# The first six slots by halves of time, the feed-forward statistics moved among the slots, and the first head prepared during the output projection

## The reference

```python
x = LN(x + hyena(x))          # LN, W_in (1536 x 512), 3-tap filter, three kinds x0 x1 v,
                              # v*x1, long convolution over T, * x0, W_out
x = LN(x + heads(ctx, x))     # 32 heads of 8 rows: products k_i*v_j of ctx, long convolution
                              # over L = 512, contracted with x
x = LN(x + ffn(x))            # bitlinear(512->2048), gelu, bitlinear(2048->512)
# bitlinear: rms = rsqrt(max(mean(w*w), eps)); w_quant = clip(round(w*rms), -1, 1) / rms
#            x_quant = clip(round(x*127/max|x|)) ...
```

## Time and profile before

| quantity | value |
|---|---|
| three timed runs | 1128.77, 1130.29, 1130.85 us |
| profiled execution, its own time | 1128.79 us |
| its span | 1127.0 us |
| mean granted TensorE clock | 0.977 |
| TensorE (matmul), VectorE, ScalarE, GpSimd busy | 93%, 72%, 52%, 52% of the span |

### The profile page before, as it was taken

The page is one execution under the profiler, slowest core; times in us unless marked ns, Lnnn a source line. Parts: engine busy times, 40 slices in busy tenths (PEclk is TensorE's granted clock), DMA queues, the critical chain, the costliest instruction groups (busy, mean ns, idle before and its releaser), DMA issues.

```text
span 1127.0 us, 16879 instructions
## 1 busy us (share of the span) xinstructions
PE 1052.1 (93%) x5316; PEld 643.6 (57%) x5316; DVE 816.0 (72%) x1531; ACT 589.4 (52%) x710; POOL 586.0 (52%) x1136
## 2 busy tenths in 40 slices
PE   1799899999999987969999999999999999999985
PEld 1455455544545533556676767676766666666652
DVE  6978786696565546857777878787878787777762
ACT  2355444203444463825565656565656565666654
POOL 2301310131000003559878787878787878788770
PEclk9899899999999998989999999999999999999997
DMA  8233445455244584332121222212131313131101
GB/s 236 93 89 113 146 140 172 147 177 177 92 133 150 150 328 147 122 112 58 57 84 58 74 67 65 74 57 83 50 89 47 93 47 93 47 90 50 47 10 29
DMA packets 95215, 115.23 MB, mean 102 GB/s; under 512 B 19584, under 2 KB 52352, under 8 KB 93632
## 3 DMA queue, kind: packets, MB, share of 16 engines
q1 hardware_dynamic: 95168, 114.63, 33.5%
HBM read 80.90 MB, written 33.70 MB: 102 GB/s over the span
## 4 chain that ended last, share of the span: by engine, by line
PE 53%; POOL 2%; ACT 1%; DVE 1%; issue 0%; POOLq 0%; DVEq 0%
PE conv_bank L1255 26%; PE hq_bank L1289 10%; PE ff_bank L1317 5%; PE back_bank L1317 5%; PE ctx_bank L1230 1%; PE ff_bank L1282 1%; PE hq_bank L1282 1%; PE back_bank L1240 1%; PE back_bank L1269 1%; PE ctx_bank L1300 1%; POOL up L1626 0%; POOL dn L1627 0%; POOL up L1629 0%; ACT o L1415 0%; POOL att L1639 0%
## 5 line engine op out<-in xcount | busy, mean ns | idle before, releaser
L752 DVE SCALAR_TENSOR_TENSOR conv_all<-u,taps,conv_all 128x1024 f32<-128x1024 f32 x96 | 126.4, 1317 | 97.9 <-ACT conv_all L624 96.1
L1255 PE MATMUL conv_bank<-block_diag 128*128 128x288 f32 x640 | 175.6, 415 | 8.8 <-PEq L265 6.0
L1255 PE MATMUL conv_bank<-kv,block_diag 128*128 128x288 f32 x640 | 171.7, 408 | 0.0
L938 POOL TENSOR_SCALAR r_rstd<-r_meanvar 128x1 f32<-128x1 f32 x32 | 13.0, 407 | 258.3 <-DVE r_meanvar L776 258.3
L616 ACT ACTIVATE u<-slot_bank,bias,unscale 128x1024 f32<-128x1024 f32 x48 | 57.9, 1207 | 164.9 <-PE slot_bank L466 161.3
L1255 PEld LDWEIGHTS conv_bank<-block_diag 128*128 128x128 f32 x640 | 120.1, 194 | 40.6 <-issue 6.6
L1626 POOL TENSOR_TENSOR up<-z_up 128x384 f32<-128x384 f32 x128 | 127.7, 998 | 27.9 <-DVE z_dn L1502 27.0
L1255 PEld LDWEIGHTS conv_bank<-kv,block_diag 128*128 128x128 f32 x640 | 117.8, 190 | 30.9 <-DVE z_dn L1502 0.5
L1490 DVE TENSOR_TENSOR z_up<-conv_bank,qx 128x512 f32<-128x512 f32 x128 | 87.7, 685 | 55.6 <-PE conv_bank L1255 43.3
L1557 DVE TENSOR_REDUCE g_max<-g 128x1 f32<-128x512 f32 x128 | 87.3, 683 | 54.8 <-ACT g L1430 54.8
L1289 PE MATMUL hq_bank<-x_lo,hq_t 128*128 128x512 f16 x512 | 124.6, 388 | 1.6 <-ACT hq_t L1397 1.6
(11 more groups left out here) (175 smaller groups left out, 1880.5 us busy)
## 6 DMA issues: line engine op xcount, KB each, us to landing
...
res<-in_x SPq DMA_DIRECT2D x32, 256.0 KB, 2.9
x_scratch<-res SPq DMA_DIRECT2D x32, 256.0 KB, 2.0
block_diag<-in_ctx SPq DMA_DIRECT2D x32, 256.0 KB, 3.4
block_diag<-ssm_scratch SPq DMA_DIRECT2D x32, 256.0 KB, 3.1
x_tok<-x_scratch SPq DMA_DIRECT2D x32, 256.0 KB, 3.7
```

Source lines behind the costliest of these rows:

```text
L752: ins = nc.vector.scalar_tensor_tensor(out=acc, in0=u[:, t0 + tap:t0 + tap + T // 2, :].rearrange("p t b -> p (t b)"), scalar=w["taps"][:, ...
L1255: last = nc.tensor.matmul(view(conv_bank[tb % 2][:, hh, :], 0, (ROW64, T // 2), (1, PAIRS)), toep[:, head.buf, (tb - sb_) * P:(tb - sb_ + ...
```

## The change

**Start.** Quad 0 is loaded first, then W_in's first group, gamma and beta, quad 1, and the small vectors, which now come as rows of 12 partitions in three DMAs and are transposed by TensorE (`turn_columns`, `copy_columns`). x of the first half is normalized by ScalarE (`norm_first`, 16 activations), with the shift made by GpSimd. The first six slots are ordered X1, V, X0 for the first eight time steps, then X1, V, X0 for the last eight; slots 0 and 3 take their columns quad by quad. Slots 0 to 2 write three separate `u` tiles, and ScalarE copies two columns of time from these for slots 4 and 5. `turn_quad(2)` and `turn_quad(3)` follow slots 1 and 2, W_in group 1 slot 4, and W_out slot 5.

**Feed-forward weights.** All eight parts are loaded and squared during the slots of the second half, in two buffers, and loaded a second time for rounding. The totals and the root are made at slots 18 to 21. Rounding is one activation on ScalarE (a multiplication and a large constant added) and one clip on VectorE; TensorE transposes the low 16 bits of the float32 in place, and the copy subtracts the offset. Transposition runs at t = 1 to 8 instead of 7 to 14.

**Output projection.** `load_res` is issued three steps ahead instead of two. ctx, Toeplitz rows and x1 of heads 0 and 1 are loaded ahead of step 0.

**First head.** ctx is transposed after t = 11, its products are made after t = 12, and the first two blocks of its convolution run at the end of `hyena_block`. `turn_x1(0)` is the first work of TensorE in `heads_block`.

The diff, cut to its core. Tables and the order of the slots:

```diff
-    def slot_of(s):
-
+    def slot_of(hf, s):
+
+        if hf == 0 and s < 2 * len(KIND_AT):
+            return 0, s % 3, s // 3
         return *PAIRS_OF_SLOTS[s // 2], s % 2
...
+        u_first = [u[:, :, :], v_ct[:, 6:T, :], view(x_quad[:, :, :, :], 0, (P, T // 2 + TAPS - 1), (1, P))]
...
-        TOTAL_AT = {3: 0, 5: 1}
-        RMS_AT = {4: 0, 6: 1}
-        ROUND_AT = {5 + i: i for i in range(2 * PARTS)}
-        PART_AT = {7 + i: i for i in range(2 * PARTS)}
-        TURN_AT = {3: 1, 10: 2, 14: 3}
-        SUM_AT = {0: 1, 5: 2, 10: 3}
...
-        SCALE_AT = {2: 1, 7: 2, 12: 3}
-        WOUT_AT = 2
+        SQUARE_AT = {1: 0, 3: 1, 5: 2, 8: 3, 10: 4, 12: 5, 15: 6, 17: 7}
+        TOTAL_AT, SUM_MATRIX_AT, MEAN_AT, INVERSE_AT = 18, 19, 20, 21
+        ROUND_AT = {21: 0, 23: 1}
+        CLIP_AT = {i - 1: i for i in range(2, 2 * PARTS)}
+        PART_AT = {1 + i: i for i in range(2 * PARTS)}
+        CTX_AT, PAIRS_AT = 11, 12
+        TURN_AT = {4: 1, 10: 2, 14: 3}
+        SUM_AT = {5: 2, 10: 3}
...
+        SCALE_AT = {3: 1, 7: 2, 12: 3}
+        WOUT_AT = 5
```

SyncE, the set-up and the second half:

```diff
+                load_quad(0)
                 load_w_in(0)
                 for src, tile in ((dram["ln_beta"], beta_bc), (dram["ln_gamma"], gamma_bc)):
                     sp.dma_start(tile, bass.AP(src.tensor, 0, [[0, P], [1, D]])).then_inc(gb_loaded, 16)
-                load_quad(0)
+                load_quad(1)
+                sp.dma_start(cols_raw[:, 0:P], dram["b_in"].rearrange("(n p) -> n p", p=P)).then_inc(cols_loaded, 16)
...
+                load_quad(2)
+                load_quad(3)
...
+                def load_stat(i):
 
                     if i < 2:
                         sp.wait_ge(x_turned, DC * (HALF * NQ - 1 + i))
+                    else:
+                        sp.wait_ge(squared, i - 1)
+                    sp.dma_start(part_target(i, part_raw[i % 2]), part_source(i)).then_inc(stat_loaded[i % 2], 16)
...
+                        load_stat(0)
+                        load_stat(1)
+                        regroup(hf, 0)
+                        load_stat(2)
+                        load_stat(3)
+                        load_stat(4)
+                        bring_back(hf, 0)
+                        load_stat(5)
+                        regroup(hf, 1)
+                        load_stat(6)
+                        load_stat(7)
+                        bring_back(hf, 1)
+                        regroup(hf, 2)
                         load_part(0)
                         load_part(1)
...
+                        bring_back(hf, 2)
+                        regroup(hf, 3)
+                        load_part(2)
+                        load_part(3)
+                        bring_back(hf, 3)
+                        for i in range(4, 2 * PARTS - 1):
                             load_part(i)
+
+
+                        sp.wait_ge(ch_full, 4 * HALF * DC)
...
+                            sp.dma_start(early["ctx_tok"][:, h, :], dram["ctx"][:, heads, :]).then_inc(early["ctx_loaded"][h], 16)
+                            sp.dma_start(early["toep"][:, h, :], toeplitz(dram, h)).then_inc(early["toep_loaded"][h], 16)
+                            sp.dma_start(early["x1_tok"][:, h, :], dram["x1_scratch"][:, heads, :]).then_inc(early["x1_loaded"][h], 16)
...
-                        if R + 2 < HALF * T:
-                            load_res(R + 2)
+                        if R + 3 < HALF * T:
+                            load_res(R + 3)
```

TensorE:

```diff
                 pe.wait_ge(ident_made, 2)
+                turn_quad(0)
+                turn_columns()
                 turn_w_in(0)
-                turn_quad(0)
+                slot(0, 0, (0,))
                 turn_quad(1)
                 for hf in range(HALF):
                     for s in range(NSLOT):
-                        slot(hf, s)
+                        slot(hf, s, (0, 1) if hf + s > 0 else (1,))
                         if hf == 0:
-                            if s == 0:
-                                turn_quad(2)
-                                turn_quad(3)
+                            if s in (1, 2):
+                                turn_quad(s + 1)
...
                     for j in range(DC):
-                        pe.wait_ge(*turn_read(KINDS + DC * NQ + j - 4))
+                        if j == 0:
+                            pe.wait_ge(w_lo_done, 2 * KINDS)
+                            pe.wait_ge(x_lo_done, DC * NQ)
...
+                def convolve_first(tb):
+
+                    if tb == 0:
+                        pe.wait_ge(early["toep_loaded"][0], 16)
+                        pe.wait_ge(early["kv_done"], 1)
+                        pe.wait_ge(part_done, 2 * 2 * PARTS)
+                    for sb_ in range(tb + 1):
+                        for hh in range(2):
+                            last = first_conv(nc, early, turn_bank[2 * tb + hh][:, :, :].rearrange("p a b -> p (a b)"), tb, sb_, hh)
+                    last.then_inc(early["conv_full"], 1)
...
+                for tb in range(2):
+                    convolve_first(tb)
```

ScalarE:

```diff
-                    if pr == 0 and n >= 2:
+                    u_here = u_first[kind] if n < 3 else u
+                    if n == 3 or n >= 6 and pr == 0:
                         act.wait_ge(conv_done, n)
+                    elif 4 <= n < 6:
+
+                        act.wait_ge(conv_done, n)
+                        act.wait_ge(u_done, kind + 1)
+                        nc.scalar.copy(u[:, T // 2:T // 2 + TAPS - 1, :], u_first[kind][:, T // 2:T // 2 + TAPS - 1, :])
...
+                def norm_first(Q):
+                    act.wait_ge(x_shifted, Q + 1)
+                    for t in range(QUAD):
+                        x = quad_buf(Q)[:, t, :]
+                        last = nc.scalar.activation(x, x, ACT.Identity, scale=rstd[:, Q, t:t + 1], bias=shift[:, Q, t:t + 1])
+                    last.then_inc(x_normed_first, 1)
...
+                    nc.scalar.activation(part_raw[i], part_raw[i], ACT.Copy, scale=rms[:, m:m + 1], bias=LOW_HALF).then_inc(rounded, 1)
...
+                norm_first(0)
+                split_hi(0)
                 scale_w_in(0)
                 copy_w_in(0)
-                split_hi(0)
+                norm_first(1)
                 split_hi(1)
+                norm_first(2)
```

VectorE:

```diff
+                def clip_part(i):
+
+                    dve.wait_ge(rounded, i + 1)
+                    nc.vector.tensor_scalar(part_raw[i], part_raw[i], LOW_HALF - 1.0, LOW_HALF + 1.0, ALU.max, ALU.min).then_inc(clipped, 1)
...
+                norm_quad_stats(0)
                 sum_beta(0)
-                norm_quad_stats(0)
+                norm_quad_stats(1)
                 measure_w_in(0)
-                norm_quad(0)
-                norm_quad_stats(1)
+                copy_columns()
+                split_lo(0)
                 split_w_lo(0)
-                split_lo(0)
-                norm_quad(1)
+                nc.vector.memset(u_first[2][:, 0:TAPS - 1, :], 0.0).then_inc(u_zeroed, 1)
+                make_biases(0)
                 norm_quad_stats(2)
                 split_lo(1)
                 norm_quad_stats(3)
-                norm_quad(2)
-                norm_quad(3)
+                sum_beta(1)
```

SyncE and TensorE in `heads_block`:

```diff
                 for i in range(4):
                     sp.wait_ge(early["res_stored"][i], 16 * (HALF * T // 4))
-                load_x1(Head(0))
-                load_x1(Head(1))
...
                     h1, h2 = n.back(1), n.back(2)
+                    if n.c == 0:
+                        turn_x1(n)
                     if n.exists():
                         convolve(n, 0, [0])
```

362 lines of the change are left out of this document (200 added, 162 removed).

## The result

The changed kernel took 1111.59, 1113.58, 1114.43 and 1115.59 us, median 1114.0, against 1130.6 for four runs of the kernel before: a ratio of 0.9858 with a 95% interval of 0.9844 to 0.9872, 16 us less. (Behind a ratio, square brackets hold its 95% interval.) The forecast was 1101, the range 1092 to 1112. The profiled execution took 1111.59 us, its span is 1109.6 us, its mean clock 0.984; it is 17.2 us shorter than the profiled execution before, where the forecast had 28.1. Measured again in a later comparison (e14) it took 1108.29 to 1116.76 in six runs, median 1112.23, ratio 0.9839 [0.9815, 0.9863].

What follows compares the result with a forecast made beforehand. TensorE was taken as the bound, busy 1052.1 of 1127.0 us, leaving its idle and lower-clock time to win. Terms 5.2 + 0 + 14.3 + 2.4 + 6.2 = 28.1 off 1128.8 gave 1100.7, said as 1101; range 1092 to 1112.

Steps and rivals of the forecast that it cites:

- Start, 5.2: Before slot 8: x loaded first and norms off VectorE let slot 8 start at 88.0 against 93.25, 5.2 us gained.
- Queued behind these waits are only later slots: After the start's waits: nothing but later slots is delayed, and V's regrouping has time, so the 5.2 us stays.
- slots of the second half, 0: Second half's slots: squares, rounding and clips moved there fit into idle engine time; cost 0, bounds 0 to 4 us.
- With a square 4.5, so nothing shows: Second half's slots: ScalarE's share with a square is 4.5 us, under TensorE's 5.2 per slot, so no cost.
- rival D: SP's in-order queue: load_stat waits for a square, regroupings start late and TensorE waits for v; 1136 us, chance 0.04.
- Output projection, 14.3: Second half's output projection: 64 out-products without the wait for the weights' total take 64.2 us; gain 14.3.
- Products out of the tail, 2.4: End of the output projection: the first head's products (0.4 and 2.28 us) leave the tail; gain 2.4.
- Three tiles of slack: Residual loads in the output projection: tiles 0 to 2 are there ahead, which spoke against rival C's loss of 8 us.
- rival C: Output projection still waits for data, parts and head loads queued ahead of residuals; loses 8 us, 1109, chance 0.09.
- First head, 6.2: After the change of block: with x1 there, VectorE's first multiplication comes after 1.9 us, not 8.1; gain 6.2, bounds 3 to 6.5.
- B: Start gives nothing or costs a little: half clock after gaps, VectorE-to-ScalarE turns in slots 3 to 5; 1108 us, chance 0.13.
- E: First head is held by another load or engine, and its 6.2 us is lost; 1107 us, chance 0.06.

Runs made afterwards that it cites:

- e1: The changed kernel with every tile of the first block at its address in the kernel before, no instruction different: 1108.66 us, ratio 0.9813.
- e2: The kernel before with its first-block tiles at the changed kernel's addresses, no instruction different: 1134.33 us, ratio 1.0028.
- e15: The changed kernel with SyncE's order at a step turned round, store_res(R) ahead of load_res(R + 3): 1107.51 us, ratio 0.98.
- e16: The changed kernel with old addresses, squares of parts 0 and 2 later, three TensorE pauses filled with transposes, and stores ahead of residual loads: 1102.19 us, ratio 0.9746.
- e17: The changed kernel with old addresses, squares of parts 0 and 2 later and three pauses filled, residual loads still ahead of stores: 1106.2 us, ratio 0.9782.
- e11: The changed kernel at the old addresses, plus 20 unread identity transposes on TensorE behind the first head's early blocks: 1105.07 us, ratio 0.9802.

## Why the prediction was wrong

The sign was right, and so were the places and the sizes of the two large terms; the sum was 28.1 and the medians had 16.6. Two steps failed: that nothing between slot 8 and the last stage gets slower, and that the residual loads have three tiles of slack. Step by step:

- **Start, 5.2.** Slot 8 came 4.5 earlier in the profile, so the chain of VectorE's terms was sound: its copies of k did stand through GpSimd's clearing, and the taps of slot 1 took 4.50 where 4.49 was taken. That profile was lucky, however. Over thirteen profiles of the new order and three of the old (89.67, 92.46, 90.22, mean 90.8) the gain at the first convolution is 3.5. What is missing goes with half clock: behind the first new pause in all thirteen (0.70 to 0.83 of the clock from 50 to 60 us), behind the second in nine (0.83 from 70 to 80), and in some already ahead of slot 0. The rule of the page "TensorE: Matmul & The Clock Gate" of the Trainium skill (What's actually happening) had been worked out as -0.8 to 1.8; the trace lies between that and my 5.2. (The bound of 9.5 with neither contention is 9.3 by its own terms, 5.2, 2.2 and 1.9.)
- **"Queued behind these waits are only later slots", and slots of the second half, 0.** This is the first step that failed. It took every transfer between slot 8 and slot 47 at the duration of before. By the table 1.7 us were lost ahead of the first half's last convolution, 2.7 across its output projection and 1.6 at the second half's last two convolutions: 6 in this profile, 9.8 in that of e14; the step to cc 1, 1.15 shorter, gave some back, so that 5.0 were gone at the last stage. Addresses are 3.3 of the 6 and 3.9 of the 9.8, the convolutions that wait; e1 and e2 put them at 3 to 5 us of the time. Most of the rest, 1.7 and 4.9, is the wait at slot 4, which belongs to the next item, and 0.9 is the longer projection, where TensorE waited 1.17 us before it could turn a quad. I had costed each instruction that the change removes, and not what a tile's removal does to those behind it.
- **"With a square 4.5, so nothing shows".** The busy time was right and a square's wait for its own load was left out: 5.32 and 7.26 us, of which up to 3.03 reached TensorE. The reason stands under rival D, "a load of 1 MB takes 3 to 4 us": in the changed kernel the loads of the parts landed 8.0 us after their issue (median of ten). My bounds of 0 to 4 held this term in the changed kernel, not in e14 (4.9).
- **Output projection, 14.3.** 13.7, with the small waits left over. Right, as long as one counts TensorE alone.
- **Products out of the tail, 2.4.** 0.2, and this is the second step that failed. "Three tiles of slack" counted when the loads may start and not what SyncE does until then: a store's landing became part of each step. I had named the queue's order for the regrouping (rival D) and for the heads' loads (rival C), and not for this pair of lines, which the diff shows. Rival C's price was of that kind, its reason was another. Turned round, it is worth 4 to 6.5 us of the time (e15 against both measurements of the changed kernel, e16 against e17), as much as the addresses or more; 2.0 of it are seen in the trace, at the change of block, and that is this term. The rest stays open.
- **First head, 6.2.** z_up 1.8 us after the change of block: right. (Before it was 7.9 by the rows; the 8.1 taken is 0.2 too much.) By the last z_up 5.2 were left (597.2 instead of 602.4), since the first z's products took 7.95 us, mostly at half clock, where they had taken 6.62 before; in e15, e11 and e16 it is 596.2, the whole 6.2. To the end it is 637.8 instead of 641.8: 4.0, because what follows the last z_up took 40.6 and not 39.4. It is the same work and took 38.0 to 40.5 in the other profiles, so that last 1.2 is chance.
- **Rivals.** B came true in part (half clock behind the new gaps), C in its symptom. E did not occur. Nor did D: no convolution waited more than 1.6 us. "An idle TensorE before a convolution in the second half would make D right" was a poor test, since it was idle there, 0.68 us, for another reason.

With the addresses and SyncE's order put right, the two squares later and three pauses filled (e16), the change gives 28.6 us. That this is near the forecast's 28.1 is in part chance: filled pauses were no term of it, and e16's gain over e17 was not traced. It does not excuse the range, which had no case for a transfer that gets slower by itself.
